# Bias rows as rounded parts on 64 partitions, counts added first, and another order on every engine of a three-layer kernel

## The chip, the cores and the metric

The kernel runs on one core of one Trainium2 chip. The metric is the time of one execution in microseconds on the device. TensorE (PE in the profile) multiplies into PSUM, VectorE (DVE), ScalarE (ACT) and GpSimd (POOL) work on SBUF, and SyncE (SP) issues the DMA transfers. Each engine runs its own list of instructions in order; semaphores are all that ties the lists together.

## The reference

Two batch rows of 128 tokens with 512 features pass through three layers, each as `x = x + layer(layernorm(x))`. Cut to what matters:

```python
# layer 1: self attention, cross attention to 2048 context rows, and an MLP, each with a layer norm
energy = einsum("bqd,bkd->bqk", Q, K)
lengths = sum(energy[:, 0] != 0, axis=-1)          # the non-zero energies of query 0
energy = where(pad | causal, -inf, energy)
z = relu(x @ fc1_w + fc1_b) @ fc2_w + fc2_b
# layer 2: RWKV-7 over the two batch rows as two steps in time
xr, xw, xk, xv, xa, xg = (x + (xprev - x) * m for m in (mu_r, mu_w, mu_k, mu_v, mu_a, mu_g))
w = exp(-exp(-softplus(-(w0 + xw @ Ww)) - 0.5))
a = sigmoid(a0 + xa @ Wa)
out = layernorm(silu(layernorm(x + att) @ Wf + bf))
# layer 3: attention with 8 heads, values and outputs picked by a top-2 gate among 5 experts
out = einsum("bthe,bthk,ekd->btd", mask_o, attn, Wo)
```

## The kernel before

All is one pass over the two batch rows; b is 0 or 1 and 0 stands for the first. Nothing loops over tiles of the output: each step is a small function (`q1`, `scores`, `gather`, `step`, `ro`, `rf`, `fg`, ...), and each engine's list is the order in which these functions are called, written out by hand. A step waits for flags, which are semaphores that count the steps of one kind in a fixed order; the order of the names in a flag is the order of the steps.

SP loads blocks of 1 MB (weights and pieces of the context) into a ring of 12 places in a fixed order. Each load waits until the block that lay in its place has been used, and holds back every load behind it. Vectors of 512 numbers (norm gains, biases) are spread over 128 partitions into `bc`: two first, twelve more in one load of 3 MB (flag `s_bc1`), and five (flag `s_bc2`) over the first ones.

The stages are: layer norm and self attention (0 to 46 us of the profiled execution), cross attention (46 to 111), the MLP (to 130), the RWKV projections (to 174), the RWKV combination and its output products `ro` and `rf` (to 209), and the last layer. In cross attention the context is held in a rounded part (ScalarE's `split`) and a remainder (VectorE's and GpSimd's `low`, which share the columns), and each product is three products of such parts in the single-pass type fp32r. `nonzero` counts non-zero energies of query 0 in four pieces, `count2` adds the four counts in PSUM and spreads the sum over the partitions, `penalty` makes a mask of it and `shut_out` adds that to the scores, of which `maxima` then takes the largest.

In the RWKV stage the blends of neighbouring tokens (`mix` on VectorE, `mix0` and `mix1` on ScalarE, two additions on GpSimd) are made one by one, each in a buffer that two projections share. Biases a0, w0 and bf come into PSUM as a product of a row of ones with the row, ahead of the projection that adds to it:

```python
            def bias(name, bk):
                mm(bank(bk), ones[0:1, :], vec(name)[0:1, :], True, False)
```

The combination is a chain of VectorE passes over [128, 512] and of tiny ones over [128, 8], with some products on GpSimd; `rs8` is a power on GpSimd of the variance that VectorE leaves in `ssq`, and its flag is called "e". The gated result ("yg") of each batch row is transposed by TensorE, copied by ScalarE and multiplied in `ro`; then come a norm ("h"), the product `rf`, a silu, a norm ("s"), the sum and the next norm ("n5"). In the last layer `sel` is a selecting matrix that GpSimd fills with a memset and two affine selects and ScalarE rounds in `select`.

## Time and profile before

| | us |
|---|---|
| median of 3 runs | 256.61 |
| lowest and highest run | 254.85, 259.63 |
| the profiled execution's own time | 256.62 |
| its span in the trace | 254.9 |
| busy in the span: TensorE, weight loads, VectorE, ScalarE, GpSimd | 232.1, 161.0, 165.0, 86.7, 87.3 |

Busy time is the time in which an engine has an instruction in work, waiting for a port included; the span runs from the first instruction to the end of the last transfer. An fp32 product appears as two matmul instructions in the rows (x8 are four products), one in fp32r as one. The granted clock is the share of TensorE's full clock.

### The profile page before, as it was taken

The numbers are of one execution on the slowest core, as the hardware profiler recorded it, in microseconds if no ns is written. First come the engines' busy times: TensorE is split into PE (matmuls) and PEld (weight loads), VectorE is DVE, ScalarE is ACT, GpSimd is POOL, SyncE is SP. The second block draws the span as 40 slices with busy tenths as digits, with TensorE's granted clock in tenths as the row PEclk, the third lists the DMA queues.
The fourth block names the chain that finished last, engine by engine and source line by source line (L and its number), as shares of the span: only waits on it lengthen the run. The fifth ranks groups of instructions, "written<-read, shape, count | busy, mean of one in ns | idle before, by whom it ended". The sixth has DMA issues, their size and how long they took to land.

```text
span 254.9 us, 3033 instructions
## 1 busy us (share of the span) xinstructions
PE 232.1 (91%) x1153; PEld 161.0 (63%) x1153; DVE 165.0 (65%) x309; ACT 86.7 (34%) x144; POOL 87.3 (34%) x81
## 2 busy tenths in 40 slices
PE   3899989999999999999899999995886789799995
PEld 3888758789888786885644433331442359599861
DVE  2234571785659786813827747779954759999962
ACT  2061123346197768121062264312101021432210
POOL 5020042220839623720402054866511213345000
PEclk9999999999999999999999999998999799999999
DMA  7999599253984199399000599000000000000002
GB/s 249 433 400 419 229 454 401 85 199 141 431 356 167 37 377 397 136 411 431 24 0 0 221 427 383 1 1 0 0 0 0 3 0 0 0 3 1 3 0 82
DMA packets 6350, 43.98 MB, mean 173 GB/s; under 512 B 832, under 2 KB 832, under 8 KB 1472
## 3 DMA queue, kind: packets, MB, share of 16 engines
q1 hardware_dynamic: 6336, 43.80, 42.6%
q8 instruction: 9, 0.15, 0.2%
q14 instruction: 5, 0.04, 0.0%
HBM read 43.27 MB, written 0.52 MB: 172 GB/s over the span
## 4 chain that ended last, share of the span: by engine, by line
PE 68%; DVE 17%; POOL 8%; issue 3%; ACT 3%; POOLq 0%; DVEq 0%
PE psum L386 63%; PE psum L390 4%; POOL slots L1661 4%; ACT slots L1407 3%; DVE slots L1099 2%; DVE slots L826 2%; POOL small L1652 1%; DVE slots L1102 1%; DVE slots L816 1%; DVE small L808 1%; DVE small L1112 1%; PE psum L502 1%; DVE ring L1151 1%; POOL small L1736 1%; DVE ring L1107 1%
## 5 line engine op out<-in xcount | busy, mean ns | idle before, releaser
L386 PE MATMUL psum<-ring,slots 128*128 128x512 f32 (+3 forms) x228 | 94.5, 562 | 6.6 <-ACT slots L1407 3.5
L386 PEld LDWEIGHTS psum<-ring,slots 128*128 128x128 f32 (+1 forms) x228 | 40.6, 196 | 51.1 <-issue 38.6
L1407 ACT ACTIVATE slots<-psum 128x512 f32<-128x512 f32 (+3 forms) x51 | 27.5, 551 | 109.4 <-PE psum L386 59.2
L386 PE MATMUL psum<-slots,ring 128*128 128x128 f32 x448 | 52.7, 277 | 2.3 <-ACT slots L1407 2.3
L386 PEld LDWEIGHTS psum<-slots,ring 128*128 128x128 f32 x448 | 51.1, 192 | 3.8 <-ACT slots L1407 3.3
L386 PE MATMUL psum<-ring_r,slots_r 128*128 128x512 f32 x192 | 46.2, 396 | 0.0
L1657 POOL TENSOR_TENSOR ring_r<-ring,ring_r 128x640 fp32r<-128x640 f32 x16 | 31.8, 2005 | 38.9 <-ACT ring_r L1407 38.9
L386 PEld LDWEIGHTS psum<-ring_r,slots_r 128*128 128x128 f32 x192 | 35.5, 188 | 9.1 <-ACT slots_r L1407 1.0
L1652 POOL TENSOR_TENSOR small<-small,mhalf 128x1 f32<-128x1 f32 x16 | 13.6, 852 | 77.1 <-DVE small L812 77.1
L1407 ACT ACTIVATE ring_r<-ring 128x2048 fp32r<-128x2048 f32 (+1 forms) x17 | 31.5, 1865 | 13.1 <-PE psum L386 8.2
L832 DVE TENSOR_TENSOR ring_r<-ring,ring_r 128x1408 fp32r<-128x1408 f32 x16 | 26.4, 1656 | 4.3 <-ACT ring_r L1407 4.3
L390 PE MATMUL psum<-ident,slots 128*128 128x128 f32 x104 | 15.6, 282 | 5.8 <-DVE slots L826 3.5
L390 PEld LDWEIGHTS psum<-ident,slots 128*128 128x128 f32 x104 | 12.3, 144 | 13.1 <-DVE slots L826 5.3
L1661 POOL TENSOR_TENSOR slots<-slots,bc 128x512 f32<-128x512 f32 x7 | 10.3, 1464 | 12.6 <-ACT slots L1407 9.4
L808 DVE BATCH_NORM_STATS2 small<-slots 128x6 f32<-128x512 f32 x16 | 11.1, 694 | 5.0 <-DMA slots<-xin 4.5
L826 DVE SCALAR_TENSOR_TENSOR slots<-slots,small,bc 128x512 f32<-128x512 f32 x10 | 10.0, 998 | 3.0 <-POOL small L1652 2.7
L1661 POOL TENSOR_TENSOR slots<-slots 128x512 f32<-128x512 f32 x8 | 10.2, 1285 | 5.0 <-ACT slots L1407 2.8
L1407 ACT ACTIVATE slots<-slots,small 128x128 f32<-128x128 f32 x22 | 7.1, 389 | 9.3 <-DVE small L873 5.5
L1407 ACT ACTIVATE slots_r<-psum 128x512 fp32r<-128x512 f32 (+1 forms) x11 | 5.9, 567 | 12.2 <-PE psum L386 6.3
L386 PE MATMUL psum<-slots 64*128 64x128 f32 (+2 forms) x68 | 9.1, 300 | 0.4 <-DVE small L837 0.4
L1407 ACT ACTIVATE slots<-psum,small 128x128 f32<-128x128 f32 (+1 forms) x12 | 6.6, 627 | 6.7 <-DVE small L924 4.8
L943 DVE SCALAR_TENSOR_TENSOR slots<-psum,small,slots 128x512 f32<-128x512 f32 x2 | 1.5, 750 | 11.3 <-PE psum L386 11.3
(158 smaller groups left out, 204.2 us busy)
## 6 DMA issues: line engine op xcount, KB each, us to landing
ring<-blocks SPq DMA_DIRECT2D x36, 1024.0 KB, 9.1
bc<-vecs SPq DMA_DIRECT2D x1, 3072.0 KB, 11.7
bc<-vecs SPq DMA_DIRECT2D x1, 1280.0 KB, 6.9
slots<-xin SPq DMA_DIRECT2D x2, 256.0 KB, 4.0
bc<-vecs SPq DMA_DIRECT2D x1, 512.0 KB, 14.2
y<-slots SPq DMA_DIRECT2D x2, 256.0 KB, 2.0
colv<-cols SPq DMA_DIRECT2D x1, 14.0 KB, 12.3
```

What stands on the lines that cost most here:

```text
L386: return t.matmul(o_, l, r, start=first, stop=last)
L390: i = t.transpose(o_[:, c * 128:(c + 1) * 128], x[:, c * 128:(c + 1) * 128], ident[:, :])
L502: i = t.matmul(bank(4 * b + n), pick_r[:, n, :], pen_r[b], start=False, stop=True, skip_group_check=True)
L808: v.bn_stats(st[b], x).then_inc(*own_v.inc())
L816: v.tensor_scalar(o, x, mv[b][:, 0:1], rs[b], ALU.subtract, ALU.mult).then_inc(*normed[b].inc(name))
L826: v.scalar_tensor_tensor(out=o, in0=tmp, scalar=rs[b], in1=vec(bname), op0=ALU.mult, op1=ALU.add).then_inc(*normed[b].inc(name))
L832: v.tensor_tensor(ring_r[:, p, 0:CUT], ring[:, p, 0:CUT], ring_r[:, high(name), 0:CUT], ALU.subtract).then_inc(*split_low.inc(name))
L1099: v.tensor_tensor(heads(N4[b] if first else Y[b]), x_, w_, ALU.mult).then_inc(*own_v.inc())
L1407: return a.activation(o, x, func, **kw)
L1652: g.tensor_tensor(rs[b], ve[b], mhalf[:, 0:1], ALU.pow).then_inc(*rstd[b].inc(name))
L1657: g.tensor_tensor(ring_r[:, p, CUT:], ring[:, p, CUT:], ring_r[:, high(name), CUT:], ALU.subtract).then_inc(*split_lowg.inc(name))
L1661: g.tensor_tensor(o, x, y, op).then_inc(*flag.inc(name))
```

## The change

The bias rows are no longer multiplied as one row by ones in fp32. ScalarE rounds the row to fp32r on 64 partitions (`row_high`), VectorE overwrites the lower 32 of these by the remainder (`row_low`), and one product with a matrix of 1/32 (`share`, written over `kidx`) adds 32 copies of each. a0 and w0 take each other's place in `bc` for it, bf that of fc2_b. The four counts of each batch row are added by VectorE (`sum_counts`) and spread by one product. And the order of steps is another one on every engine and in SP's queue. The core of the diff, with the flags' new orders and steps that only swap left out:

```diff
...
+W0, A0, BF, FREE = BCAST.index("w0"), BCAST.index("a0"), 0, BCAST.index("fc2_b")
+row_parts = {"a0": (W0, 0), "w0": (A0, 64), "bf": (FREE, 0)}
...
     eng.dma_start(X[0], xin[0, :, :]).then_inc(s_x[0], 16)
+    fetch("k1")
+    eng.dma_start(X[1], xin[1, :, :]).then_inc(s_x[1], 16)
     fetch("q1")
-    eng.dma_start(X[1], xin[1, :, :]).then_inc(s_x[1], 16)
-    fetch("k1")
-    fetch("ct00")
+    fetch("ct01")
+    eng.dma_start(colv[:, :], cols).then_inc(s_cols, 16)
     fetch("v1")
-    fetch("ct01")
     eng.dma_start(bc[:, 0:2, :], spread(0, 2)).then_inc(s_bc0, 16)
-    fetch("k2")
     fetch("q2")
     fetch("ct03")
     fetch("ct02")
+    eng.dma_start(bc[:, 2:FIRST_BC, :], spread(2, FIRST_BC)).then_inc(s_bc1, 16)
+    fetch("k2")
+    fetch("ct00")
     fetch("ct10")
-    eng.dma_start(bc[:, 2:FIRST_BC, :], spread(2, FIRST_BC)).then_inc(s_bc1, 16)
+    fetch("ct11")
+    fetch("c02")
     fetch("ct12")
-    fetch("ct11")
-    eng.dma_start(colv[:, :], cols).then_inc(s_cols, 16)
     fetch("c01")
-    fetch("c02")
     fetch("ct13")
-    fetch("v2")
-    fetch("c03")
     fetch("c00")
     fetch("c10")
+    fetch("c03")
+    fetch("v2")
     fetch("c12")
     fetch("f2")
     fetch("c11")
+    fetch("f1")
+    fetch("c13")
+    fetch("rv")
+    s.wait_ge(*used("c12"))
+    fetch("fg")
+    fetch("ra")
+    fetch("rr")
+    fetch("fq")
+    fetch("fk")
     fetch("rk")
-    fetch("c13")
-    fetch("f1")
-    fetch("rv")
-    fetch("rr")
+    fetch("fo")
     fetch("rg")
     s.wait_ge(*used("c13"))
     fetch("rw")
-    fetch("ra")
...
     s.wait_ge(*normed[0].at("n4"))
     s.wait_ge(*normed[1].at("n4"))
     eng.dma_start(bc[:, 0:len(BCAST) - FIRST_BC, :], spread(FIRST_BC, len(BCAST))).then_inc(s_bc2, 16)
-    fetch("fk")
-    fetch("fq")
...
-    fetch("fo")
-    s.wait_ge(*used("c11"))
...
     def bias(name, bk):
-        mm(bank(bk), ones[0:1, :], vec(name)[0:1, :], True, False)
+        i, p = row_parts[name]
+        s.wait_ge(*rows_a.at("share"))
+        s.wait_ge(*rows_v.at(name))
+        mm(bank(bk), share[p:p + 64, :], bc_r[p:p + 64, i, :], True, False)
...
     def count2(b):
 
         bk = 3 if b else 7
-        for n in range(4):
-            s.wait_ge(*counted[b].at(str(n)))
-            i = mm(psum[:, bk, 0:1], ones[0:1, :], cnt4[b][0:1, n:n + 1], n == 0, n == 3)
-        i.then_inc(*prod[b].inc("n2"))
+        s.wait_ge(*counted[b].at("sum"))
+        mm(psum[:, bk, 0:1], ones[0:1, :], cnt[b][0:1, :], True, True).then_inc(*prod[b].inc("n2"))
...
     q2(1)
+    scores(0, 2)
+    k2(1)
     count2(0)
-    k2(1)
     shut_out(0)
...
     gather(0, 0)
+    count2(1)
     turn_p(0, 3)
     turn_p(0, 2)
-    count2(1)
...
     turned_rows(0, "x2", Z[0], 3)
+    s.wait_ge(*p_low[0].at("3"))
+    s.wait_ge(s_bc1, 16)
+    bias("a0", 1)
...
     turned_rows(0, "n4", N4[0], 0)
     f2(1)
+    s.wait_ge(*p_low[1].at("3"))
+    s.wait_ge(*evict[1].at("relu"))
+    bias("a0", 6)
...
-    s.wait_ge(*p_low[1].at("3"))
-    s.wait_ge(*evict[1].at("relu"))
-    bias("a0", 6)
...
-    s.wait_ge(s_bc2, 16)
-    s.wait_ge(*evict[0].at("r"))
-    bias("bf", 0)
     step(1, "v", 4, 5, wait=evict[1].at("k"))
-    s.wait_ge(*evict[1].at("r"))
-    s.wait_ge(s_bc2, 16)
-    bias("bf", 4)
+    step(1, "g", 5, 6, wait=evict[1].at("th"))
     step(0, "g", 4, 1, wait=evict[0].at("th"))
-    step(1, "g", 5, 6, wait=evict[1].at("th"))
...
+    s.wait_ge(s_bc2, 16)
+    s.wait_ge(*evict[0].at("r"))
+    bias("bf", 0)
...
+    s.wait_ge(*evict[1].at("r"))
+    s.wait_ge(s_bc2, 16)
+    bias("bf", 4)
...
+    def sum_counts(b):
+        for m in four:
+            s.wait_ge(*counted[b].at(m))
+        v.tensor_reduce(cnt[b][0:1, :], cnt4[b][0:1, :], AX.X, ALU.add).then_inc(*counted[b].inc("sum"))
...
+    def row_low(name):
+        i, p = row_parts[name]
+        low_rows = slice(p + 32, p + 64)
+        s.wait_ge(*rows_a.at(name))
+        v.tensor_tensor(bc_r[low_rows, i, :], vec(name)[low_rows, :], bc_r[low_rows, i, :],
+                        ALU.subtract).then_inc(*rows_v.inc(name))
...
+    low("ct00")
+    row_low("w0")
     k2_split(0)
     add1(1)
...
+    nonzero(0, 3)
+    low("ct10")
     nonzero(0, 2)
-    nonzero(0, 3)
+    sum_counts(0)
+    low("ct12")
+    penalty(0)
+    k2_split(1)
+    maxima(0)
...
     p_split(1, 3)
-    weigh2(1)
-    norm2(0)
     done2(0)
     low("c13")
+    row_low("a0")
...
     centre_v(0)
     mix("a", 1)
+    keys(0)
+    s.wait_ge(*sq_a[1].at("kx"))
+    v.tensor_reduce(keep["rn"], heads(sc_[1]), AX.X, ALU.add).then_inc(*own_v.inc())
+    keys_c(1)
     s.wait_ge(*sq_a[0].at("vc"))
     v.tensor_reduce(keep["m00"], heads(TMP[0]), AX.X, ALU.add).then_inc(*own_v.inc())
-    s.wait_ge(*sq_a[1].at("kx"))
-    v.tensor_reduce(keep["rn"], heads(sc_[1]), AX.X, ALU.add).then_inc(*own_v.inc())
-    mix("r", 3)
-    s.wait_ge(*own_v.now())
-    v.tensor_scalar(keep["m00"], keep["m00"], 1.0 / 64, None, ALU.mult).then_inc(*own_v.inc())
-    keys_c(1)
-    s.wait_ge(*own_v.now())
-    v.tensor_scalar(keep["rn"], keep["rn"], 1e-24, None, ALU.max).then_inc(*own_v.inc())
     keys(1)
     read_keys(0)
     sum_read(0)
     s.wait_ge(*own_v.now())
+    v.tensor_scalar(keep["m00"], keep["m00"], 1.0 / 64, None, ALU.mult).then_inc(*own_v.inc())
+    mix("r", 3)
+    mix("v", 4)
+    s.wait_ge(*own_v.now())
     v.tensor_tensor(ssq[0], keep["m00"], ss[0], ALU.mult).then_inc(*own_v.inc())
     s.wait_ge(*own_v.now())
     v.tensor_tensor(ssq[0], ssq[0], ss[0], ALU.mult).then_inc(*own_v.inc())
     s.wait_ge(*own_v.now())
     v.tensor_scalar(ssq[0], ssq[0], 0.00064, None, ALU.add).then_inc(*rk_v[0].inc("e"))
...
-    v.reciprocal(keep["rn"], keep["rn"]).then_inc(*rk_v[1].inc("rn"))
     s.wait_ge(*rk_g[1].at("c3"))
     v.tensor_reduce(keep["c3"], heads(th[1]), AX.X, ALU.add).then_inc(*own_v.inc())
+    s.wait_ge(*rk_g[0].at("sc"))
+    v.tensor_tensor(ys[0], vc[0], sc_[0], ALU.mult).then_inc(*rk_v[0].inc("y"))
...
+    centre_v(1)
+    s.wait_ge(*rk_g[1].at("c1"))
+    v.tensor_reduce(keep["c1"], heads(w1), AX.X, ALU.add).then_inc(*own_v.inc())
+    s.wait_ge(*sq_a[1].at("vc"))
+    v.tensor_reduce(keep["m11"], heads(TMP[1]), AX.X, ALU.add).then_inc(*own_v.inc())
...
     v.tensor_reduce(keep["m01"], heads(c2t), AX.X, ALU.add).then_inc(*own_v.inc())
-    s.wait_ge(*own_v.now())
-    v.tensor_tensor(heads(ys[1]), heads(vc[0]), over(keep["al"], 64), ALU.mult).then_inc(*own_v.inc())
...
-    v.tensor_reduce(keep["m11"], heads(TMP[1]), AX.X, ALU.add).then_inc(*own_v.inc())
+    sum_read(1)
     s.wait_ge(*own_v.now())
...
-    s.wait_ge(*own_v.now())
-    v.tensor_tensor(ssq[1], ssq[1], keep["al"], ALU.mult).then_inc(*own_v.inc())
-    s.wait_ge(*rk_g[0].at("sc"))
-    v.tensor_tensor(ys[0], vc[0], sc_[0], ALU.mult).then_inc(*rk_v[0].inc("y"))
...
     s.wait_ge(*rk_v[0].at("y"))
     s.wait_ge(*rk_g[0].at("pv"))
     v.tensor_tensor(ys[0], ys[0], pv[0], ALU.add).then_inc(*rk_v[0].inc("yb"))
     s.wait_ge(*own_v.now())
-    v.tensor_scalar(ssq[1], ssq[1], 0.0, 0.00064, ALU.max, ALU.add).then_inc(*rk_v[1].inc("e"))
...
     s.wait_ge(*evict[0].at("g"))
     s.wait_ge(*rk_v[0].at("yb"))
     v.scalar_tensor_tensor(out=ys[0], in0=gt[0], scalar=1.0, in1=ys[0], op0=ALU.add,
                            op1=ALU.mult).then_inc(*rk_v[0].inc("yg"))
     s.wait_ge(*own_v.now())
+    v.tensor_tensor(heads(ys[1]), heads(vc[0]), over(keep["al"], 64), ALU.mult).then_inc(*own_v.inc())
+    s.wait_ge(*own_v.now())
+    v.tensor_tensor(ssq[1], ssq[1], keep["al"], ALU.mult).then_inc(*own_v.inc())
+    s.wait_ge(*own_v.now())
+    v.tensor_tensor(ssq[1], ssq[1], keep["m11"], ALU.add).then_inc(*own_v.inc())
+    row_low("bf")
+    s.wait_ge(*own_v.now())
     v.tensor_tensor(ys[1], ys[1], sc_[1], ALU.add).then_inc(*own_v.inc())
+    s.wait_ge(*own_v.now())
+    v.tensor_scalar(ssq[1], ssq[1], 0.0, 0.00064, ALU.max, ALU.add).then_inc(*rk_v[1].inc("e"))
     s.wait_ge(*own_v.now())
...
+    affine(1, "h", hn[1], TMP[1], "norm_b")
     silu(0)
-    affine(1, "h", hn[1], TMP[1], "norm_b")
...
+    norm(1, "n5", Z[1], X[1])
+    ranks(0)
     value_gate(0)
     expert(0, 0, True)
...
+    def share_out():
+        s.wait_ge(*const.at("ones"))
+        for b in range(2):
+            s.wait_ge(*energy_in[b].at("nb1"))
+        act(share[:, :], ones[:, :], ACT.Copy, scale=1.0 / 32).then_inc(*rows_a.inc("share"))
+
+    def row_high(name, loaded_):
+
+        i, p = row_parts[name]
+        s.wait_ge(*loaded_)
+        act(bc_r[p:p + 64, i, :], vec(name)[p:p + 64, :], ACT.Copy).then_inc(*rows_a.inc(name))
...
+    split("ct02")
     pickers()
-    exp1(0)
     out(1, "q1", bcols(T10, 1), quarters(5))
+    row_high("w0", (s_bc1, 16))
+    out(1, "v1", Vs[1], bank(5))
     copy_turned(0, "x1", T8, 0)
-    out(1, "v1", Vs[1], bank(5))
-    split("ct02")
     exp1(1)
     out(0, "q2", bcols(T10, 0), quarters(1))
+    row_high("a0", (s_bc1, 16))
+    split("ct00")
     out(0, "k2", bcols(T12_r, 0), quarters(2))
     split("ct03")
+    copy_turned(1, "x1", T8, 4)
     split("ct10")
-    copy_turned(1, "x1", T8, 4)
+    split("ct12")
+    out(1, "q2", bcols(T10, 1), quarters(5))
...
     mix0("v", 2)
-    tanh(0, "a", "th", th[0], 1)
     out(0, "k", kt[0], bank(2))
     copy_turned(1, "n4", T8, 4)
     out(0, "v", vt[0], bank(3))
+    mix1("w", 2)
+    mix0("r", 3)
+    out(1, "k", kt[1], bank(5))
+    s.wait_ge(*rk_g[1].at("kx"))
+    act(sc_[1], kx, ACT.Square).then_inc(*sq_a[1].inc("kx"))
...
     s.wait_ge(*rk_v[0].at("km"))
     act(TMP[0], vc[0], ACT.Square).then_inc(*sq_a[0].inc("vc"))
-    mix0("r", 3)
-    out(1, "k", kt[1], bank(5))
-    mix1("w", 2)
-    s.wait_ge(*rk_g[1].at("kx"))
-    act(sc_[1], kx, ACT.Square).then_inc(*sq_a[1].inc("kx"))
-    tanh(1, "a", "th", th[1], 6)
-    mix0("g", 4)
-    s.wait_ge(*rk_v[1].at("c"))
-    act(th[1], th[1], ACT.Copy, scale=0.5, bias=0.5).then_inc(*sq_a[1].inc("a"))
     out(0, "r", rt[0], bank(0))
     s.wait_ge(*const.at("wbias"))
     s.wait_ge(*prod[1].at("w"))
     act(w1, bank(7), ACT.Tanh, scale=0.5).then_inc(*evict[1].inc("w"))
+    mix0("g", 4)
+    s.wait_ge(*x2b_g[0].at("x2b"))
+    s.wait_ge(*x2b_g[1].at("x2b"))
+    row_high("bf", (s_bc2, 16))
     s.wait_ge(*evict[1].at("w"))
     act(w1, w1, ACT.Exp, bias=wbias[:, :], scale=WC).then_inc(*sq_a[1].inc("wexp"))
     out(1, "r", rt[1], bank(4))
+    mix1("g", 5)
...
     silu(0)
+    select()
     copy_turned(1, "h", T10, 7)
+    silu(1)
     copy_turned(0, "n5", T8, 1)
-    silu(1)
...
+    g.iota(kidx[:, :], pattern=[[1, 128]], base=0, channel_multiplier=0,
+           allow_small_or_imprecise_dtypes=True).then_inc(*const.inc("kidx"))
     deviation(0, "x")
+    g.iota(kidx4[:, :], pattern=[[1, 512]], base=0, channel_multiplier=512,
+           allow_small_or_imprecise_dtypes=True).then_inc(*const.inc("kidx4"))
     deviation(1, "x")
-    low("ct00")
+    low("ct01")
+    g.memset(causal[:, :], 0.0).then_inc(*own_g.inc())
...
+    s.wait_ge(*own_g.now())
+    s.wait_ge(*rk_v[0].at("sb"))
+    mul(heads(sc_[0]), heads(vec("lnx_w")), over(rs8[0], 64), rk_g[0], "sc")
+    s.wait_ge(*rk_g[1].at("a"))
+    s.wait_ge(*evict[1].at("r"))
+    mul(th[1], th[1], rt[1], rk_g[1], "c3")
+    s.wait_ge(*mixed[1].at("g"))
+    mixg = MIX[1][1].rearrange("p (c n) -> p c n", c=4)
+    mul(mixg, mixg, bcols(T8, 1), mixed_g, "g", ALU.add)
     s.wait_ge(*rk_v[0].at("vc"))
     s.wait_ge(*rk_v[0].at("sb"))
     g.tensor_tensor(heads(pv[0]), heads(vt[0]), over(sbs[0], 64), ALU.mult).then_inc(*own_g.inc())
     s.wait_ge(*sq_a[1].at("wexp"))
...
+    mul(pv[0], pv[0], vec("lnx_b"), rk_g[0], "pv", ALU.add)
...
+    s.wait_ge(*prod[1].at("w"))
+    g.memset(sel, 0.0).then_inc(*own_g.inc())
     s.wait_ge(*own_g.now())
-    s.wait_ge(*rk_v[0].at("sb"))
-    mul(heads(sc_[0]), heads(vec("lnx_w")), over(rs8[0], 64), rk_g[0], "sc")
-    s.wait_ge(*mixed[1].at("g"))
-    mixg = MIX[1][1].rearrange("p (c n) -> p c n", c=4)
-    mul(mixg, mixg, bcols(T8, 1), mixed_g, "g", ALU.add)
+    mul(pv[1], pv[1], vec("lnx_b"), rk_g[1], "pv", ALU.add)
+    for base in (0, -8):
+        s.wait_ge(*own_g.now())
+        i = g.affine_select(out=sel, in_=sel, compare_op=ALU.not_equal, fill=-1.0, base=base,
+                            pattern=[[-1, 8], [0, 128]], channel_multiplier=1)
+        i.then_inc(*(const.inc("sel") if base else own_g.inc()))
     s.wait_ge(*rk_v[1].at("e"))
     g.tensor_tensor(rs8[1], ssq[1], mhalf[:, 0:8], ALU.pow).then_inc(*rk_g[1].inc("rs"))
-    s.wait_ge(*own_g.now())
-    mul(pv[1], pv[1], vec("lnx_b"), rk_g[1], "pv", ALU.add)
...
-    s.wait_ge(*prod[1].at("w"))
-    g.memset(sel, 0.0).then_inc(*own_g.inc())
...
-    for base in (0, -8):
-        s.wait_ge(*own_g.now())
-        i = g.affine_select(out=sel, in_=sel, compare_op=ALU.not_equal, fill=-1.0, base=base,
-                            pattern=[[-1, 8], [0, 128]], channel_multiplier=1)
-        i.then_inc(*(const.inc("sel") if base else own_g.inc()))
...
```

## Rows read from the trace of the kernel before

**Rows 1.** Windows by stage of core 0: us of each engine, instructions, clock.
```profile
core 0: us, PE busy (x) PEld busy (x) DVE busy (x) ACT busy (x) POOL busy (x), PEclk, DMA share, GB/s
...
46.26:111.10 64.84, 64.64 (x333) 52.60 (x332) 48.75 (x71) 36.03 (x36) 32.18 (x16) 1.00 0.61 241
...
173.70:209.00 35.30, 26.82 (x68) 12.46 (x69) 24.30 (x47) 5.16 (x9) 10.07 (x10) 0.90 0.00 0
209.00:238.30 29.30, 26.98 (x223) 24.50 (x221) 28.33 (x50) 8.71 (x22) 12.03 (x13) 1.00 0.00 1
```

**Rows 2.** Timeline of TensorE: start us, us, engine, line, operation, tiles, count.
```profile
61.40 1.05 PE L386 MATMUL psum<-small,ones 1*128 1x1 f32 x8
...
66.15 1.19 PE L502 MATMUL psum<-slots_r 4*128 4x512 f32 x4
...
168.93 1.12 PE L386 MATMUL psum<-bc,ones 1*128 1x512 f32 x2
169.99 3.70 PE L386 MATMUL psum<-ring,slots 128*128 128x512 f32 x8
```

**Rows 3.** Chain that ended last, first 4 us: start us, us, engine, tile, line.
```profile
2.12 0.29 POOL causal L1678
...
2.62 0.49 POOL kidx L1682
```

**Rows 4.** Timeline: first norm, first scores, and a later affine step.
```profile
33.69 2.11 DVE L826 SCALAR_TENSOR_TENSOR slots<-slots,small,bc 128x512 f32<-128x512 f32 x1 [0.44 <-POOL small L1652]
...
46.26 8.44 PE L386 MATMUL psum<-ring_r,slots_r 128*128 128x512 f32 x36
...
197.55 0.75 DVE L826 SCALAR_TENSOR_TENSOR slots<-slots,small,bc 128x512 f32<-128x512 f32 x1
```

**Rows 5.** Timeline of SP: four loads of the first twelve us, merged.
```profile
4.80 1.95 SPq L319 DMA_DIRECT2D ring<-blocks  x4
```

**Rows 6.** DMA issues at 5.4 and 5.8 us: KB each, us to landing.
```profile
ring<-blocks SPq DMA_DIRECT2D x1, 1024.0 KB, 19.6
...
ring<-blocks SPq DMA_DIRECT2D x1, 1024.0 KB, 21.6
```

**Rows 7.** Timeline behind the projections, all engines.
```profile
172.81 1.04 POOL L1764 TENSOR_TENSOR slots<-slots,small 128x512 f32<-128x512 f32 x1
...
173.39 1.00 DVE L1301 TENSOR_TENSOR slots<-slots,small 128x512 f32<-128x512 f32 x1
...
176.57 5.16 PE L386 MATMUL psum<-ring,slots 128*128 128x512 f32 x8 [2.88 <-POOL slots L1661]
...
179.39 0.16 DVE L1329 TENSOR_SCALAR small<-small 128x8 f32<-128x8 f32 x1
...
181.88 1.68 DVE L1340 TENSOR_TENSOR slots<-slots,small 128x512 f32<-128x512 f32 x1 [0.28 <-POOL small L1772]
...
184.47 0.69 DVE L1027 SCALAR_TENSOR_TENSOR slots<-slots 128x512 f32<-128x512 f32 x1
...
186.40 0.60 PE L390 MATMUL psum<-ident,slots 128*128 128x128 f32 x4
```

**Rows 8.** Timeline of the later stages, all engines.
```profile
199.69 5.40 PE L386 MATMUL psum<-ring,slots 128*128 128x512 f32 x8 [0.69 <-ACT slots L1407]
...
206.68 0.69 DVE L1047 SCALAR_TENSOR_TENSOR slots<-slots,psum 128x512 f32<-128x512 f32 x1 [2.47 <-ACT slots L1407]
...
214.60 0.94 POOL L1782 MEMSET ring<- 16x1024 f32 x1
...
214.80 3.06 DVE L816 TENSOR_SCALAR slots<-slots,small 128x512 f32<-128x512 f32 x1
...
227.93 2.84 POOL L1793 TENSOR_SCALAR_AFFINE_SELECT ring<-ring 16x1024 f32<-16x1024 f32 x2
```

**Rows 9.** Windows of 2 us in the later stages, columns as in the first group.
```profile
200.00:202.00 2.00, 2.00 (x3) 0.68 (x2) 1.53 (x3) 0.00 (x0) 0.37 (x1) 0.51 0.00 0
```

**Rows 10.** Groups by form: busy us, mean ns, idle before, releaser.
```profile
L1407 ACT ACTIVATE ring_r<-ring 16x1024 fp32r<-16x1024 f32 x1 | 1.1, 1056 | 2.6 <-POOL ring L1793 2.6
```

310 lines of the change are left out of this document (145 added, 165 removed).

## The prediction

> **What bounds the kernel now.** I read the windows by stage first, and in each the busy time of the engines against its length [rows 1]. The reader is to see that the limit changes. In cross attention (46.3 to 111.1 us) TensorE is busy in 64.64 of 64.84 us: there, what TensorE no longer does is won. Between 173.7 and 209.0 it is busy in 26.82 of 35.30, and from 209.0 to 238.3 VectorE is busy in 28.33 of 29.30: there a shorter product is worth nothing unless VectorE gets its data sooner. Then I read the timeline for single products, for the ends of the stages, and for the instructions of VectorE that last longer than their kind.
>
> **The products that change.** A bias product goes from 168.93 to 169.99, 1.06 us [rows 2]. The new one is a single pass of 512 columns on 64 rows. The nearest row is the penalty product on 4 rows, four in 1.19, so 0.30 each; the other end is 1.06, nothing won. I take 0.30, since the form (one pass of 512 columns) is that of the row: 0.76 saved, five times. The counts took 1.05 for four; one takes 0.26, so 0.79 is saved twice [rows 2]. Together 5.4 us of TensorE. Where do they lie?
> The two counts lie in cross attention: 1.6 won. But `count2(0)` now stands behind `k2(1)`, so that `penalty(0)` on VectorE, until now under `k2(1)`, stands open between count and `shut_out` (0.5, estimated as one short pass of VectorE). `sum_counts` hides under `k2(1)`. `k2(1)` also has to wait for ScalarE's split of ct12, whose load is now queued in SP behind c02, and GpSimd does its share of c01 ahead of c00, which `gather(0, 0)` needs first: I put 0.8 on these two. Cross attention wins 0.3.
> The first "a0" product now stands where TensorE waits for ScalarE's copy anyway, so it costs nothing and wins nothing: at its old place the chain of the norms decided. Nor do the "bf" products win by themselves: behind them TensorE waited 2.88 us for GpSimd [rows 7].
>
> **Self attention.** `ones`, which TensorE's first products need, comes off GpSimd ahead of the causal select and kidx4: 0.29 and 0.49 us leave that chain [rows 3], 0.8. The affine step of the first norm at 33.69 took 2.11 us, where the same instruction takes 0.75 at 197.55 [rows 4]; one of GpSimd's subtractions ran beside it, and that one is now done earlier. 1.35 more. I take 2.0 of the 2.15 for the start of the scores, 46.26 until now [rows 4], provided that ScalarE isn't held up. It may be: `row_high("w0")` waits for the 3 MB of vectors, and behind it in ScalarE's order stand `out(1, "v1")`, the copy of x1 and so `q2(0)`. That load now stands behind ct02 in SP's queue, with as many bytes ahead of ct02 as q2, the second of the four issued from 4.80 on, had ahead of it [rows 5]. q2 was issued near 5.4 and took 19.6: ct02 lands near 25. Two loads issued 0.5 us apart landed 19.6 and 21.6 after their issue, 2.5 us per MB [rows 6], so the 3 MB land at 32.4. ScalarE then comes to the copy at 33.6, and TensorE has the transposes of x1 done at 34.1. Covered by 0.5 us; each us that the load is later costs one. k2 lands at 35 and ct00 at 37.5, before they are read (39 and 40). Of the later loads, fk waits for `f1(1)`, fo for `f2(1)`, and rk, rg, rw, rf and ro stand behind them; by the same pace rk lands at 133 and is read at 135. No wait. The copies and subtractions of the bias rows on ScalarE and VectorE (an ordinary pass each) hide under TensorE, but for "bf".
> So the second `v2` and the first projections come 2.3 us earlier than before.
>
> **The end of the projections, where the change is decided.** TensorE had v's second product done at 168.93 [rows 2]. 2.3 earlier, two biases at 0.76 and one "bf" of 1.06 less ahead of it: 4.9. But the blend for r on VectorE now stands behind `keys_c(1)`, `keys(1)`, `read_keys(0)` and `sum_read(0)`, and `out(0, "r")` behind the tanh, the scale and the square on ScalarE; laying these out, I find it 1.5 us later than TensorE could take it. Left are 3.3 to 3.4. GpSimd's blend for g comes early now, so the wait of 2.88 shrinks to about 0.7.
> What follows hangs on the variance of batch row 1 ("e"), which ended at 179.55 [rows 7]. Between v's second product and e, VectorE's order now has the sum c1, `sum_read(1)`, the gate of `ys[0]`, `row_low("bf")` and the sum of `ys[1]`, and one product ("y" of batch row 0) less: four passes of 0.69 net [rows 7], 2.8 us. Hence 179.55 - 3.3 + 2.8 = 179.05. From e to the last gate it took 5.6 (to 185.16), with one product of 1.68 held up by GpSimd's addition of lnx_b [rows 7]; that is done earlier now: 4.6. The transposes of "yg" for row 1 can start at 183.7, if nothing else holds VectorE. Before, they started at 186.40, held up by TensorE itself [rows 7].
> But GpSimd does hold VectorE. A product of two SBUF operands issued at 173.39 ended at 174.39, 0.54 after the GpSimd instruction from 172.81 to 173.85 [rows 7]. And the change moves GpSimd's memset of `sel` (0.94 us) and both its selects (2.84 us [rows 8]) ahead of `rs8[1]`, into this stretch: up to 3.5 of these 3.8 us. So 183.7 to 187.2. I take 186.0, nearer to the upper end, as the row shows a VectorE instruction waiting out the GpSimd instruction beside it. The Trainium skill (SBUF — State Buffer, Who interferes with whom) says that a VectorE instruction with two SBUF inputs contends with a GpSimd instruction that reads SBUF, not with one that only writes it. By it the memset would block nobody, and the upper end would be some 0.9 lower, 186.3; the instruction issued at 214.80, during the memset, lasted 3.06 us [rows 8], past the memset's end by 2.3, and no row tells what held it at first.
>
> **Behind it.** Before, `rf(1)` started at 199.69 [rows 8], 13.3 after 186.40; `affine(1, "h")` now comes before `silu(0)`, so TensorE's wait for the second h goes. But `select` (1.06 us [rows 10]) now stands on ScalarE between `silu(0)` and the copy of that h. Counted from the start of the yg transposes: 12.2, not 13.3. `rf(1)` took 5.40 us, at a granted clock of 0.51 [rows 8, 9], the lower of the two levels (1.2 GHz); its sisters take 3.70 at 2.4 GHz [rows 2]. TensorE still idles about 2 us before it, so I keep 5.40. Until `silu(1)` on VectorE at 206.68 [rows 8] it then takes 6.4 instead of 7.0, as ScalarE's tanh no longer follows the copy of n5. 186.0 + 12.2 + 6.4 = 204.6, 2.1 us earlier than before.
> The last stage has the same work. `fg(1)` comes before the scores, but VectorE then still has an expert, the values and the maxima to do; without the selects beside it, 0.3 is won. The tail of TensorE is the same.
> Sum against the profiled execution: span 254.9 - 2.1 - 0.3 = 252.5, and 1.7 lie around it (256.62 in all, the median being 256.61): 254.2; I say 254.0.
>
> **Rivals.**
> A. VectorE isn't held up by the moved GpSimd work: the transposes start at 183.7, and with the shorter gap TensorE does `rf(1)` in 3.70. 2.3 and 1.7 less, of which the chain through `silu(0)` gives back 0.6: 250.6. For it: the moved instructions touch 16 partitions only; against it the row at 173.39.
> B. The other side: a VectorE step in this stretch waits for two GpSimd instructions and not for one. The one issued at 214.80 lasted 3.06, far past the end of the instruction that it met [rows 8]. GpSimd has hardly a gap from 162 to 180 in the new order; four further waits of 1.3 (between the 1.04 of the row at 172.81 and the 1.42 of one select) give 5.2 us: 259.2. It makes the kernel slower as soon as the transposes start after 188.6.
> C. The lower clock strikes twice. TensorE idles some 7 us before the first yg. Should a second product on the path run at 5.40 (`ro(1)` or `fg(0)`), 1.7 more each: 255.7 to 257.4.
> D. The new products take as long as the old: five times 0.76 more, of which only the two ahead of `r` in batch row 1 were counted, and that one waits for its blend anyway: 254 to 255. The time can't tell it, the rows can.
>
> **How the numbers follow.** Forecast (with D): 0.46, from 252 to 256. A: 0.27, from 249 to 251.5. C: 0.16. B: 0.11, half of it above 258.5. The range 249.8 to 258.5 leaves out the lower part of A and the upper half of B. About 2% (251.5 and 261.7) is what a measurement of this kernel tells from no change. Faster by more: A and a little of the forecast's lower edge, 0.29; slower by more: the end of B, 0.05; within: 0.66.
>
> **What would show it.** The bias rows should read about 0.3 us and come five times. The first scores should start near 44.3; if ScalarE's copy of x1 starts after 34.5, the load was late. The second v product should end near 165.6, and the two yg transposes start near 180 and 186. If the second starts by 184, A holds; after 188, B. A granted clock near 0.5 in more than one product behind 186 is C. The prediction is wrong if a wait that I call covered shows up before 130, or if the last stage's 48 us behind `silu(1)` change by more than 1.

## The result and the profile after

The changed kernel takes 263.0 us (median of four runs, 260.86 to 263.2), the kernel before 258.12 over the four runs now shown of it; the ratio is 1.026, with an interval of 1.020 to 1.033. Forecast were 254.0 and no change that can be told. (Executions of one and the same kernel lie in groups a few us apart here, and a ratio in this document leaves out those of either kernel that are more than 1.5% above its fastest.) The profiled execution took 263.2 us, its span is 261.4.

TensorE's timeline of the changed kernel, with the columns of [rows 2] (start, length, engine, line, operation, tiles, count, and in brackets the wait ahead and who ended it):

```profile
8.12 9.41 PE L394 MATMUL psum<-slots,ring 128*128 128x128 f32 x64 [0.69 <-ACT slots L1433]
...
48.38 4.84 PE L394 MATMUL psum<-ring_r,slots_r 128*128 128x512 f32 x20 [0.93 <-DVE slots_r L910]
...
68.97 1.19 PE L511 MATMUL psum<-slots_r 4*128 4x512 f32 x4 [1.88 <-DVE slots_r L931]
...
70.09 10.04 PE L394 MATMUL psum<-ring_r,slots_r 128*128 128x512 f32 x36
...
133.80 0.66 PE L398 MATMUL psum<-ident,slots 128*128 128x128 f32 x4 [1.64 <-DVE slots L825]
...
159.71 0.49 PE L394 MATMUL psum<-bc_r,share 64*128 64x512 f32 x1
...
164.76 7.11 PE L394 MATMUL psum<-ring,slots 128*128 128x512 f32 x16 [0.92 <-DVE slots L1015]
...
188.06 1.12 PE L398 MATMUL psum<-ident,slots 128*128 128x128 f32 x4 [8.68 <-DVE slots L1349]
...
189.86 5.37 PE L394 MATMUL psum<-ring,slots 128*128 128x512 f32 x8 [0.69 <-ACT slots L1433]
...
195.59 0.66 PE L398 MATMUL psum<-ident,slots 128*128 128x128 f32 x4
...
207.63 3.70 PE L394 MATMUL psum<-ring,slots 128*128 128x512 f32 x8 [1.66 <-ACT slots L1433]
```

Read it against the forecast, point by point along TensorE's work:

| start, us | before | forecast | after | lost against the forecast, in the step |
|---|---|---|---|---|
| first scores | 46.26 | 44.3 | 46.24 | 1.9 |
| n4 of row 0 transposed | 129.59 | 127.3 | 133.80 | 4.6 |
| end of v's second product | 168.93 | 165.6 | 171.87 | -0.2 |
| variance "e" of row 1 done | 179.55 | 179.05 | 190.64 | 5.3 |
| yg of row 1 transposed | 186.40 | 186.0 | 195.59 | -2.0 |
| `rf(1)` | 199.69 | 198.2 | 207.63 | -0.2 |
| `silu(1)` on VectorE | 206.68 | 204.6 | 212.83 | -1.2 |
| end of the span | 254.9 | 252.5 | 261.4 | 0.7 |

The fourth column less the third grows by what the last one says; the sum is 8.9. Three steps carry it: the opening, cross attention, and VectorE's chain up to e. The rest went as forecast or better, but for 0.7 at the end. The new products themselves are cheap: a bias reads 0.49 us where 1.12 did [rows 2], the count 0.38 where four products took 1.05.

In cross attention three rows stand out: the wait of 0.93 at 48.38, the wait of 1.88 at 68.97, and the 36 score products behind it, which read 10.04 where before they read 8.48. The windows over that stretch, and over the first `ro`, show the granted clock (the column behind POOL's):

```profile
core 0: us, PE busy (x) PEld busy (x) DVE busy (x) ACT busy (x) POOL busy (x), PEclk, DMA share, GB/s
...
70.00:72.00 2.00, 2.00 (x6) 1.56 (x6) 1.80 (x1) 0.00 (x0) 0.33 (x1) 0.60 0.42 176
...
190.00:192.00 2.00, 2.00 (x3) 0.97 (x4) 1.20 (x3) 0.00 (x0) 1.27 (x1) 0.50 0.00 0
```

At 190 it is the lower of the two levels, 1.2 GHz (0.50); in the window from 70 it is that level for most of the time (0.60). Each time TensorE had just waited, 1.88 and 8.68 us. Who made it wait is in the timeline of all engines. First cross attention:

```profile
44.06 4.95 POOL L1701 TENSOR_TENSOR ring_r<-ring,ring_r 128x640 fp32r<-128x640 f32 x2 [9.36 <-ACT ring_r L1433]
...
45.67 1.93 DVE L994 TENSOR_TENSOR bc_r<-bc,bc_r 32x512 fp32r<-32x512 f32 x1
...
65.30 5.03 POOL L1701 TENSOR_TENSOR ring_r<-ring,ring_r 128x640 fp32r<-128x640 f32 x3 [11.15 <-ACT ring_r L1433]
...
67.13 1.79 DVE L931 TENSOR_SCALAR slots_r<-kidx,psum 4x512 fp32r<-4x512 f32 x1 [1.38 <-PE psum L394]
```

`row_low("w0")` (line 994) reads 1.93 us, though it touches 32 partitions; the same pass reads 0.68 where GpSimd is idle. GpSimd's remainders ran beside it from 44.06 to 49.01. `penalty(0)` (line 931), which was 0.48 before, reads 1.79; GpSimd's next remainders ran from 65.30 to 70.33. Both stand ahead of what TensorE needs next. Then the stretch ahead of e:

```profile
173.59 2.60 POOL L1705 TENSOR_TENSOR slots<-slots 128x512 f32<-128x512 f32 x2
...
173.68 1.19 DVE L1317 TENSOR_TENSOR small<-small 128x8 f32<-128x8 f32 x1
...
174.79 0.67 DVE L1022 TENSOR_REDUCE small<-slots 128x8 f32<-128x512 f32 x1
...
175.50 0.72 DVE L1024 TENSOR_SCALAR small<-small 128x8 f32<-128x8 f32 x1
...
176.15 1.26 POOL L1705 TENSOR_TENSOR slots<-slots,bc 128x512 f32<-128x512 f32 x1
...
176.25 1.71 DVE L1029 TENSOR_TENSOR slots<-slots,small 128x512 f32<-128x512 f32 x1
...
182.21 0.94 POOL L1816 MEMSET ring<- 16x1024 f32 x1
...
182.84 0.69 DVE L1336 TENSOR_TENSOR slots<-slots,small 128x512 f32<-128x512 f32 x1
...
184.61 2.77 POOL L1821 TENSOR_SCALAR_AFFINE_SELECT ring<-ring 16x1024 f32<-16x1024 f32 x2
...
185.12 1.05 DVE L1341 SCALAR_TENSOR_TENSOR small<-small 128x8 f32<-128x8 f32 x1
...
186.41 0.99 DVE L1346 TENSOR_TENSOR small<-small 128x8 f32<-128x8 f32 x1
...
190.47 0.17 DVE L1361 TENSOR_SCALAR small<-small 128x8 f32<-128x8 f32 x1
...
194.37 0.69 DVE L1048 SCALAR_TENSOR_TENSOR slots<-slots 128x512 f32<-128x512 f32 x1
```

A product of eight numbers per partition, 0.17 us by itself, reads 1.19, 1.05 and 0.99; one of 512, 0.69 by itself, reads 1.71. Each ends 0.02 to 0.55 us after a GpSimd instruction does; this waiting is called the hold below. Nine instructions between 171.59 and 187.40 are longer than their kind, by 7.6 us together; before, in the same part of the work, four were, by 2.1. The reduction at 174.79, beside GpSimd as well, is not.

These steps stand ahead of both gates. The first yg can be transposed only when its gate (line 1349, 0.68 us from 187.32 on) is done, and that is what TensorE's 8.68 us wait for. The second gate, which hangs on e, is the row at 194.37: it ends at 195.06, 0.5 ahead of the second transposes at 195.59, which follow `ro(0)` and a bias on TensorE without a wait. So in this execution the second yg is set by the first gate and by `ro(0)` at 5.37, and e is late beside it but not what TensorE waits for.

### The profile page after: what moved, and what is told of

The parts are those of the page before. It is cut to its first block, busy times and chain, and to the rows that moved or that the text cites. A ratio compares the mean times of both kernels' runs of the same rounds, so it can differ in the third digit from the quotient of the medians.

```text
span 261.4 us, 3018 instructions
## 1 busy us (share of the span) xinstructions
PE 231.9 (89%) x1136; PEld 161.4 (62%) x1136; DVE 169.1 (65%) x314; ACT 87.9 (34%) x148; POOL 87.0 (33%) x81
## 4 chain that ended last, share of the span: by engine, by line
PE 71%; DVE 15%; POOL 5%; ACT 4%; issue 3%; POOLq 0%; DVEq 0%; ACTq 0%
PE psum L394 65%; PE psum L398 4%; ACT slots L1433 3%; POOL slots L1705 2%; POOL small L1696 2%; DVE small L817 1%; DVE ring_r L841 1%; PE psum L511 1%; DVE slots L1015 1%; ACT ring_r L1433 1%; DVE slots_r L931 1%; DVE slots L1339 1%; DVE slots L1029 1%; POOL small L1783 1%; DVE slots L835 1%
## 5 line engine op out<-in xcount | busy, mean ns | idle before, releaser
L394 PE MATMUL psum<-ring,slots 128*128 128x512 f32 (+3 forms) x228 | 93.0, 555 | 5.4 <-ACT slots L1433 4.1
L394 PEld LDWEIGHTS psum<-ring,slots 128*128 128x128 f32 (+1 forms) x228 | 39.8, 193 | 47.9 <-issue 39.5
L394 PE MATMUL psum<-slots,ring 128*128 128x128 f32 x448 | 54.8, 283 | 2.4 <-ACT slots L1433 2.4
L394 PEld LDWEIGHTS psum<-slots,ring 128*128 128x128 f32 x448 | 53.2, 198 | 4.1 <-ACT slots L1433 3.3
L394 PE MATMUL psum<-ring_r,slots_r 128*128 128x512 f32 x192 | 48.8, 407 | 1.1 <-DVE slots_r L910 0.9
L1701 POOL TENSOR_TENSOR ring_r<-ring,ring_r 128x640 fp32r<-128x640 f32 x16 | 30.3, 1908 | 55.6 <-ACT ring_r L1433 55.6
L835 DVE SCALAR_TENSOR_TENSOR slots<-slots,small,bc 128x512 f32<-128x512 f32 x10 | 7.5, 751 | 5.5 <-POOL small L1696 5.5
L915 DVE TENSOR_SCALAR_CACHE_REDUCE slots<-psum 1x512 f32<-1x512 f32 x8 | 5.3, 676 | 7.7 <-PE psum L394 7.7
L394 PE MATMUL psum<-slots 64*128 64x128 f32 (+2 forms) x68 | 10.1, 303 | 0.3 <-ACT slots L1433 0.2
L394 PEld LDWEIGHTS psum<-slots 64*128 64x128 f32 (+1 forms) x68 | 7.5, 188 | 2.3 <-issue 1.6
```

The lines of the kernel that those rows point to most:

```text
L394: return t.matmul(o_, l, r, start=first, stop=last)
L835: v.scalar_tensor_tensor(out=o, in0=tmp, scalar=rs[b], in1=vec(bname), op0=ALU.mult, op1=ALU.add).then_inc(*normed[b].inc(name))
L915: v.tensor_scalar(PT[b][0:1, n * 512:(n + 1) * 512], psum[0:1, 4 * b + n, :], 0.0, 0.0, ALU.not_equal, ALU.add, accum_out=cnt4[b][0:1, n:n ...
L1701: g.tensor_tensor(ring_r[:, p, CUT:], ring[:, p, CUT:], ring_r[:, high(name), CUT:], ALU.subtract).then_inc(*split_lowg.inc(name))
```

## The experiments

**The new products alone, in the old order.** The kernel before with `row_high`, `row_low`, `share_out`, `sum_counts` and the new `bias` and `count2` of the diff, placed so:

```diff
 split("c00")
+row_high("w0", (s_bc1, 16)); row_high("a0", (s_bc1, 16)); share_out()
 ...
 low("c13")
+row_low("w0"); row_low("a0")
 ...
 gated(1)
+row_low("bf")
 ...
 turned_rows(0, "h", hn[0], 3)
+bias("bf", 0)
```

> The kernel before in its own order on every engine, with the new bias rows and the summed counts alone: the rounded rows, remainders and the 1/32 matrix are made behind the context splits, where ScalarE and VectorE have room, the remainder of bf while VectorE waits for ro(0), and both bf products stand behind the transposes of h. Theory (the orders cost the time, the new products save it): no stage is longer than before, each bias row reads about 0.5 us and each count 0.4; TensorE reaches v's second product 2 to 3 us earlier, of which the chain of VectorE behind it keeps 1 to 3: 253.5 to 255.5 against 256.6 before. Rival (the new products bring the loss with them, by their passes on ScalarE and VectorE or by the waits for them): 258 or more, with waits of TensorE ahead of the bias products or counts.

Measured: 0.999 of the kernel before, 0.993 to 1.004. The part of the theory on the stages holds, the time doesn't follow. TensorE's timeline:

```profile
174.18 6.07 PE L392 MATMUL psum<-ring,slots 128*128 128x512 f32 x8 [5.15 <-POOL slots L1701]
...
184.91 0.60 PE L396 MATMUL psum<-ident,slots 128*128 128x128 f32 x4
...
237.32 3.52 PE L392 MATMUL psum<-ring,slots 128*128 128x65 f32 x16
```

v's second product ends 3.4 us earlier, and the second yg is transposed at 184.91, 1.5 earlier. But the wait for GpSimd's blend is now 5.15, not 2.88, and g's second product behind it reads 6.07, not 5.16. And from 237 on products in the last stage read up to twice what they do before, at a granted clock of 0.50: some 3 us, in a stage whose instructions and order are the same as before. So the new products don't cost the loss. Of the 3.4 us that they free on TensorE, 1.0 goes into the longer wait for GpSimd's blend, and the lower clock takes 0.9 at g and some 3 in the last stage.

**Two steps moved in cross attention.**

```diff
 count2(0)
-shut_out(0)
 scores(1, 0)
+shut_out(0)
 ...
-row_low("w0")
 k2_split(0)
 ...
 low("c13")
+row_low("w0")
```

> The changed kernel with two steps moved: the remainder of w0 on VectorE from ahead of the remainder of k2(0) to where that of a0 is made, and the penalty's product of batch row 0 behind the first scores of row 1. Theory (these two waits of TensorE, 0.93 and 1.88, and the lower clock from 70 to 73 are what cross attention lost): the penalty's product ends its row of scores with no wait, the first 36 score products read 8.5 instead of 10.0, and the second n4 is transposed 3 to 4 us earlier than 133.8; 259.5 to 260.5 in all. Rival (the loads or VectorE's remainders are the bound there): the waits come back at the next step of the scores, and less than 1.5 us is won by 133.8.

(The n4 of this text is that of batch row 0, the one at 133.80.) Measured: 1.012, 1.004 to 1.020, from three executions of 261.28 to 261.72; the profiled one took 267.38, and in it that n4 comes at 135.56, 1.8 later. In the rows of this one the rival holds. The first wait is gone: 24 score products run through without one. The other comes back at the next steps (0.87 and 2.06), since the penalty is held just as long (1.74), and `k2_split(1)` and, behind `maxima(0)`, the remainder of ct11 stand behind it on VectorE. Timeline of all engines:

```profile
65.85 1.74 DVE L931 TENSOR_SCALAR slots_r<-kidx,psum 4x512 fp32r<-4x512 f32 x1 [1.45 <-PE psum L394]
...
75.60 5.53 PE L394 MATMUL psum<-ring_r,slots_r 128*128 128x512 f32 x16 [2.06 <-DVE ring_r L841]
```

The time doesn't decide between the two. Against the changed kernel's 1.026 the ratio is 3.7 us better, about what the theory forecast; the medians, 261.52 and 263.0, are 1.5 apart; and the execution that left the rows is 6 us longer than the three behind the ratio. The rows show where the wait went; what the two moves are worth is open.

**GpSimd's remainders kept off the penalty.** A wait is added on GpSimd; `row_low("w0")` is moved as above.

```diff
 low("ct03")
+s.wait_ge(*counted[0].at("pen"))
 low("ct11")
```

> The changed kernel with the remainder of w0 made later on VectorE, as in the run before, and with a wait on GpSimd: its remainders of ct11, ct12 and ct10 begin only behind the penalty of batch row 0. Theory (the penalty is held by GpSimd's remainder beside it): the penalty reads 0.48 us and not 1.79, TensorE waits 0.5 to 0.6 us ahead of the penalty's product and not 1.88, the score products behind it run at the full clock, 8.5 to 9.0 us, unless they now wait for GpSimd's late remainders (then the wait names GpSimd); the second n4 at 130.5 to 132 instead of 133.8. Rival (the penalty is slow by itself at this place): 1.7 again.

Measured: 1.021, 1.013 to 1.028. TensorE's timeline, and VectorE's:

```profile
8.13 7.41 PE L394 MATMUL psum<-slots,ring 128*128 128x128 f32 x64 [0.69 <-ACT slots L1433]
...
44.25 5.72 PE L394 MATMUL psum<-ring_r,slots_r 128*128 128x512 f32 x24
...
64.43 1.19 PE L511 MATMUL psum<-slots_r 4*128 4x512 f32 x4 [0.57 <-DVE slots_r L931]
...
65.55 10.23 PE L394 MATMUL psum<-ring_r,slots_r 128*128 128x512 f32 x36
...
130.23 0.66 PE L398 MATMUL psum<-ident,slots 128*128 128x128 f32 x4 [1.65 <-DVE slots L825]
```

```profile
63.90 0.48 DVE L931 TENSOR_SCALAR slots_r<-kidx,psum 4x512 fp32r<-4x512 f32 x1 [1.39 <-PE psum L394]
```

The penalty reads 0.48 and the wait 0.57: the theory on the hold is right. The score products behind it read 10.23 all the same, with no wait among them and a granted clock of 0.50 from 66 to 68. A wait of 0.57 was followed by the lower clock here. n4 comes at 130.23, 3.6 earlier than in the changed kernel; 2.0 of it is the opening (below), 1.6 the two edits. In time, 1.021 beside 1.026, no gain can be told.

**The selecting matrix back in the last stage.** GpSimd's memset and both selects move behind `deviation(1, "n5")` and `expert(1, 3, ...)`, ScalarE's `select()` behind `fk_out(1)`, as before.

> The changed kernel with GpSimd's memset and both selects of sel, and ScalarE's rounding of it, at the places that they had before, in the last stage. Theory (a VectorE instruction with two SBUF inputs waits out the GpSimd instruction beside it): the two tiny VectorE instructions of 1.05 and 0.99 us read 0.17 to 0.3, the gate of the first yg comes 1.5 to 1.8 us earlier, and with it the rest as long as ro(0) follows it; the last stage gives back 0.3 to 1.0; 260.5 to 262 in all against 263.0. Rival (VectorE is held by its own chain and not by GpSimd): the same chain, no change before 195, and 263 to 264.

Measured: 1.022, 1.015 to 1.029. VectorE's timeline, then TensorE's:

```profile
185.44 0.17 DVE L1346 TENSOR_TENSOR small<-small 128x8 f32<-128x8 f32 x1
...
185.52 0.69 DVE L1349 SCALAR_TENSOR_TENSOR slots<-slots 128x512 f32<-128x512 f32 x1
```

```profile
188.06 6.07 PE L394 MATMUL psum<-ring,slots 128*128 128x512 f32 x8 [0.69 <-ACT slots L1433]
```

The tiny product reads 0.17 where it was 0.99, and the gate of the first yg comes at 185.52 instead of 187.32: the theory, as far as VectorE goes. (One hold comes in new: GpSimd's addition of lnx_b now runs earlier, and the tiny step at 182.27 beside it reads 1.26.) In time the rival's figure came: `ro(0)` reads 6.07 instead of 5.37, so that the second yg gains 1.1 (194.50), and behind a wait of 2.57 for n5 the gate's product reads 4.65 instead of 2.95. The clock took it back.

**GpSimd's passes cut short.**

```diff
-mul(w1, w1, km[0], rk_g[1], "w")
+mul(w1[:, 0:64], w1[:, 0:64], km[0][:, 0:64], rk_g[1], "w")
 ... and six more in the same way
```

> The changed kernel with seven of GpSimd's passes behind the projections cut to an eighth of their columns (the rest of those columns is left out): both products for c1, the bonus product of row 1, the covariance, both additions of lnx_b and the two selects of sel. Their number, order and waits stay. Theory (VectorE's instructions with two SBUF inputs, and its tiny ones, wait out the GpSimd instruction beside them): from the end of v's second product to the variance flag e of row 1 it takes 12.5 to 13.5 us, not 18.8; the tiny products read 0.17 and the full ones 0.69; TensorE's wait of 8.68 shrinks to about 3.5, and the whole is 3.5 to 5.5 us shorter than the changed kernel: 257.5 to 259.5 against 263.0. Rival (VectorE simply has more passes ahead of e in the new order, and waits for results): at least 17 us from v's end to e, and no more than 1.5 us won in all.

Measured: 1.000, 0.996 to 1.004. Against the changed kernel that is nearly 7 us by the two ratios and 5.7 by the two medians (257.32 and 263.0), a little more than expected; the profiled span is 258.1. From the end of v's second product (171.83) to e (184.70) it takes 12.87 us, not 18.77. VectorE's timeline:

```profile
173.67 0.24 DVE L1317 TENSOR_TENSOR small<-small 128x8 f32<-128x8 f32 x1
...
174.75 0.69 DVE L1029 TENSOR_TENSOR slots<-slots,small 128x512 f32<-128x512 f32 x1
...
184.53 0.17 DVE L1361 TENSOR_SCALAR small<-small 128x8 f32<-128x8 f32 x1
```

The product of eight reads 0.24 where it was 1.19 beside a full pass, that of 512 reads 0.69 where it was 1.71. VectorE has the same passes in the same order as in the changed kernel, so its own work isn't what makes the chain long. Nor is it a wait for GpSimd's results: in the changed kernel VectorE has no gap of more than 0.2 us between 171.59 and e. So 5.9 us of the chain are the hold. TensorE's wait of 8.68 is 2.74 here (forecast about 3.5), but `ro(0)` behind it reads 6.75 at the lower clock, and of the 5.9 the second yg keeps 5.0 (190.55).

**The opening, twice.** Once GpSimd's opening in the order before (ones last again), once q1 ahead of k1 again, in SP's queue, on TensorE and on VectorE.

> The changed kernel with GpSimd's opening in the order of the kernel before, so that the ones, and with them TensorE's first products, come 1.1 us later. Theory A (TensorE's rate is what the first products set: begun earlier, they run at the half rate for longer): the first 64 weight products read 7.4 instead of 9.4 us, and v1(0) and the transposes of x1(0) start no later than in the changed kernel, though the start is later. Theory B (the second weight block's landing holds them): the 64 products read 8.3, that is, they end at the same time as in the changed kernel, and the later start is lost nowhere else.

> The changed kernel with the two first weights in the order of the kernel before (q1 loaded and multiplied ahead of k1, k1's copy on VectorE behind the transposed x of row 1). Theory (with k1 first, something of that order keeps the first products at the half rate): the 64 first weight products read 7.4 us instead of 9.4, and the transposes of x1(0) start 1 to 2 us earlier than 35.86. Rival (the rate is not a matter of which weight is first): 9.1 to 9.5 again.

The first took 263.81 in its one run, and its 64 weight products read 9.09, above the 7.4 and 8.3 of the theories, so neither explains it. The second took 265.75, they read 7.41, and the transposes of x1(0) start at 34.83, as its theory has it. But that theory falls with two other rows: in the run with the kept-off remainders k1 is first and the 64 products read 7.41, and in the next run below q1 is first, the opening is the kernel before's to the instruction, and they read 9.40. So it is not the order.

**Two steps of the new order around the second h, on the first of these runs.**

```diff
-silu(0)
 affine(1, "h", hn[1], TMP[1], "norm_b")
+silu(0)
 ... on ScalarE:
-copy_turned(0, "n5", T8, 1)
 silu(1)
+copy_turned(0, "n5", T8, 1)
```

> The kernel before in its own order with the new bias rows and counts, as in the first of these runs, and two steps of the changed kernel's order: the affine step of the second h ahead of the first silu on VectorE, and ScalarE's tanh for the second silu ahead of its copy of n5. Theory (TensorE's wait of 2.07 for the second h goes and nothing takes its place): rf(1) starts 2.0 us earlier than in that run, the second silu 1.8, and the whole 1.5 to 2.0: 0.985 to 0.993 of the kernel before. Rival (the lower clock or the last stage gives it back): rf(1) earlier, but 0.995 to 1.002.

Measured: five executions took 261.31 to 262.65, among them the profiled one (261.93), and one took 257.36; the median of the kernel before on the same chip is 257.26. TensorE's timeline:

```profile
9.23 9.40 PE L392 MATMUL psum<-slots,ring 128*128 128x128 f32 x64 [0.69 <-ACT slots L1429]
...
197.83 3.70 PE L392 MATMUL psum<-ring,slots 128*128 128x512 f32 x8 [0.31 <-ACT slots L1429]
...
204.12 0.72 PE L396 MATMUL psum<-ident,slots 128*128 128x128 f32 x4 [2.59 <-DVE slots L821]
...
205.52 5.70 PE L392 MATMUL psum<-ring,slots 128*128 128x400 f32 x8 [0.69 <-ACT slots L1429]
```

From the second yg (186.78) to `rf(1)` it takes 11.05 us where it took 13.29: 2.2 won, the theory. Then TensorE waits 2.59 for n5 (0.89 in that run), and the gate's product reads 5.70, not 2.95. In these rows the rival holds. The one execution that lies near the kernel before's median puts the whole where the rival had it, and whether its gate's product was slow too isn't on record.

**Idle products in TensorE's waits.** On the first run, and then on the one just told:

```diff
 step(0, "g", 4, 1, wait=evict[0].at("th"))
+for _ in range(5):
+    mm(bank(0), ones[:, :], vec("r_k"), True, True)
 step(1, "g", 5, 6, wait=evict[1].at("th"))
 ... and in the second of the two also:
 rf(1)
+for _ in range(2):
+    mm(bank(6), ones[:, :], vec("r_k"), True, True)
```

> The new bias rows and counts in the order of the kernel before (the first of these runs), with five products of ones and r_k into a free bank, whose result nothing reads, between g's products of the two rows, where TensorE waited 5.15 us for GpSimd's blend and then ran g's second product in 6.07 at the lower clock. Theory (the wait costs nothing by itself there, the lower clock behind it does): g's second product reads 3.70 and starts within 0.2 us of 174.2, the first yg is transposed at 178 and not at 180.1, the second at 183 and not at 184.9, and 1.5 to 2.1 us are kept to the end: 0.988 to 0.994 of the kernel before. Rival (the clock falls in another place instead, or VectorE sets the second yg): the second yg at 184.5 or later, 0.996 to 1.002.

> The run with the two steps of the changed kernel's order around the second h, where the norm ahead of the first n5 left TensorE waiting 2.59 us and the gate's product behind it read 5.70 at the lower clock; now with the five idle products before g's second product, and two more behind rf(1). Theory (the gain of 2 us at rf(1) was given back by the lower clock): the gate's first product reads 2.95, and both gains stand: 0.980 to 0.988 of the kernel before. Rival (the last stage is VectorE's, and what comes earlier waits there): the gate's product at 2.95, but no more than 1 us better than the run with five idle products alone.

Measured: 0.993 (0.991 to 0.995) and 0.990 (0.982 to 0.999): both are below the kernel before and the changed one. But the first ratio rests on four executions of seven (252.78 to 253.02, the others 257.29 to 257.81), the second on two of twelve (251.05 and 253.55, the others 255.12 to 258.38), and the profiled ones are among the others. TensorE's timeline of the first, then of the second:

```profile
173.79 3.67 PE L392 MATMUL psum<-ring,slots 128*128 128x512 f32 x8 [0.89 <-POOL slots L1704]
...
182.35 0.66 PE L396 MATMUL psum<-ident,slots 128*128 128x128 f32 x4
...
194.35 0.66 PE L396 MATMUL psum<-ident,slots 128*128 128x128 f32 x4 [2.07 <-DVE slots L834]
...
195.69 5.18 PE L392 MATMUL psum<-ring,slots 128*128 128x512 f32 x8 [0.24 <-ACT slots L1432]
```

```profile
201.52 2.95 PE L392 MATMUL psum<-ring,slots 128*128 128x400 f32 x8 [0.69 <-ACT slots L1434]
```

g's second product reads 3.67 instead of 6.07 and the second yg comes at 182.35 instead of 184.91: up to there the theory of the first. In this execution it isn't kept. `rf(1)`, behind the same wait of 2.07 as in the run of the new products alone, reads 5.18 where it read 3.70 there, later products run at the lower clock too, and the span is 255.6 against 256.1: the rival's clock that falls in another place instead. The four short executions, at a mean granted clock of 0.99, are where the theory put them. In the second run TensorE waits 0.87 for n5 and the gate's product reads 2.95, but by the two ratios the whole is only 0.6 us better than the first, which the intervals can't tell from nothing; that fits the rival's bound. In its profiled execution the products from 234 to 244 run at the lower clock again.

## Why the prediction was wrong

**What held.** The new products cost 0.49 and 0.38; I had taken 0.30 (of 0.30 to 1.06) and 0.26, so a bias saves 0.6, not 0.76. The load of vectors landed at 32.24 (forecast 32.4), and ScalarE's copy of x1 was not held up. From the n4 to the end of v's second product 0.2 better than forecast, with the late blend for r in the rows (a wait of 0.92) and GpSimd's blend no longer waited for. From the second yg to `rf(1)` 12.0, forecast 12.2.

**The step that failed most** is "four passes of 0.69 net, 2.8 us" from v's second product to e. The count of passes was right: with GpSimd's passes cut short the stretch takes 12.87, against the 13.4 that it makes. The size was wrong by 5.3, because I let GpSimd hold VectorE only behind e, and only by the memset and the selects. In fact the blend for g, both products for c1, the bonus, the covariance and the additions of lnx_b now fill GpSimd from 168 to 187 with a few gaps, and a step of VectorE with two SBUF inputs that meets one of them waits it out, the tiny ones too. That is near rival B, whose price was 5.2 (four waits of 1.3) where the row of the table has 5.3. But B let a step wait for two GpSimd instructions; in the rows nine steps wait, each for the one beside it, 0.45 to 1.06 us longer than their kind. That the sums agree is in part luck. I gave B 0.11 because of held rows only the one at 173.39 spoke for it [rows 7]; three more stood in the same part of the trace before, tiny steps of 0.6 to 0.9 us instead of 0.17, and I had not counted them:

```profile
171.88 0.78 DVE L1297 TENSOR_TENSOR small<-small 128x8 f32<-128x8 f32 x1
...
174.43 0.89 DVE L1303 TENSOR_TENSOR small<-small 128x8 f32<-128x8 f32 x1
...
175.95 0.59 DVE L1307 SCALAR_TENSOR_TENSOR small<-small 128x8 f32<-128x8 f32 x1
```

The part of the hold that I had put behind e (2.3) was then not there: hence the 2.0 that came back.

**The path** was wrong too. "What follows hangs on the variance of batch row 1" and "the two yg transposes start near 180 and 186": the first started at 188.06. Its gate stands behind the same held steps, and it, with `ro(0)` behind it, set the second at 195.59; the gate that hangs on e was ready 0.5 us earlier. The two paths lie so close that the forecast of the second from e alone would have missed by little; the hold delays both.

**Cross attention** failed in two steps. "The copies and subtractions of the bias rows hide under TensorE": `row_low("w0")` stands ahead of `k2_split(0)` and is held by 1.2 us, so TensorE waits 0.93. "0.5, estimated as one short pass": the penalty is that pass only if GpSimd is idle; with the remainders beside it TensorE waits 1.88. The run with the wait on GpSimd gives 0.57, about the price that I had taken. The lower clock on the products behind costs 1.6 more, and in the run with the wait on GpSimd it came as well. These are 3.9 of the 4.6; the rest I have not followed.

**The opening** was forecast for the shorter of two forms that an execution can have. In the run with the kept-off remainders the scores start at 44.25 (forecast 44.3). The changed kernel's profiled execution has 64 first products of 9.41 instead of 7.41, and that is its whole 1.9. Whether the new order makes the longer form likelier is open (last section).

**The clock.** I had rival C, the lower level on a second product of the path, at 0.16, and only for the stretch behind yg. There it came on `ro(0)` (5.37); on `rf(1)`, where I had kept it (5.40), it did not (3.70 behind a wait of 1.66). And it came in cross attention, where I had no term for it. In the profiled executions of four runs, those of the new products alone, of the kept-off remainders, of the selecting matrix and of the two steps around h, it took back 0.7 to 3 us of what was won. It should have been a term of the sum and not only a rival; what sets it is not shown.

The Trainium skill (SBUF — State Buffer, Who interferes with whom) has both halves of the hold. A VectorE instruction with two SBUF inputs contends with a GpSimd instruction that reads SBUF, not with one that only writes; the row at 182.84, such a product beside the memset of 182.21, reads 0.69, so the trace agrees; the memset would have been no part of the upper end. It also says that `tensor_scalar` can, under conditions on its operands, go into a mode that takes the shared port pair, and that a reduction on this chip never contends. The penalty and the tiny scaling at 175.50 (0.72), both with one SBUF input, are held; the reduction at 174.79 isn't: the trace agrees again.

## What to carry to other kernels

Before moving a GpSimd instruction into a stretch in which VectorE is on the path, count every VectorE instruction there with two SBUF inputs, and every scaling, at the end of the GpSimd instruction beside it, however small it is; a tiny product costs as much as a large one. Look in the trace before for tiny instructions that are longer than their kind: they are the price list. And where TensorE will come earlier than its data, the time won is idle time, and the product behind it may run at the lower clock (6.07 us instead of 3.70 at g): a gain on TensorE is a gain only if what it waits for comes earlier too. Products that nobody reads, put into that wait, kept the next one at 3.67 in both runs that had them (5.16 to 6.07 in three without); but in the profiled execution of the first the lower clock then came in another place, and only four executions of seven came out below the kernel before's shortest.

## What was not expected of the hardware

The first 64 weight products read 7.41 us in some executions and 9.1 to 9.4 in others: 7.41 in the kernel before, in the new products alone, with idle products, with q1 first and with the kept-off remainders, 9.1 to 9.4 in the changed kernel and five others, among them one whose opening is that of the kernel before instruction for instruction. In the longer ones products of 128 columns read some 0.2 us until 12 to 13 us instead of 0.115, as the warm-up products do, while the granted clock column reads 1.00. What decides it is open; it is 2 us, nearly as much as the change was forecast to win. The longer form came in four of the five kernels profiled with the changed kernel's opening and in one of the five with that of the kernel before, too few to tell whether the order has a part in it. The times have a step of the same size: at a mean granted clock of 0.993 the kernel before took 254.7 to 254.9 us in some executions and 257.1 to 257.3 in others, the changed kernel at 0.974 took 260.86 and 263.2. That this is the opening is not shown, as of these executions only the one of 263.2 left a trace; if it is, some 2 us of what the changed kernel lost can be of this kind.

A wait of 0.57 us ahead of a product was followed by the lower clock, and waits of 0.9 to 2.1 elsewhere weren't; the same 2.07 ahead of the second h was followed by 3.70 in one run and by 5.18 in another. So no length of wait that separates the two cases can be read from these rows, and which of a kernel's late products will run at 1.2 GHz could not be forecast from its waits.
